# A linear attention stage on one Trainium2 core: layer-norm statistics step by step, and GpSimd's sums of two steps behind one norm

## The chip, the cores and the metric

The kernel runs on one core of a Trainium2 chip, in one launch. The metric is the device time of that launch in microseconds (us). A core has a matrix engine (TensorE, PE in the profile; PEld is its weight load), VectorE (DVE), ScalarE (ACT), GpSimd (POOL) and a queue for DMAs (SP). Each engine runs its own instruction stream in order; semaphores tie the streams together.

## The reference

The program is six blocks on x, 8 batches of 512 tokens with 128 channels: a gated feed-forward with 4-bit blocks, softmax attention, the feed-forward again, a mixture of experts, a linear attention of six layers, and the mixture of experts again. The change lies in the linear attention alone:

```
for l in range(6):
    h = layernorm(x) * gamma[l] + beta[l]          # over the channels
    q, k, v = split(h @ w_qkv[l])
    q = softmax(q, over the 512 tokens);  k = softmax(k, over the channels)
    context = k v^T  (per batch, over channels)
    x = (q applied to context) @ w_out[l] + b_out[l] + x
```

Ahead of it the program applies one more layer norm to x; the stage works on that copy in the tile `ya` and adds x back in the last layer.

## The kernel before, in words

`linear_attn_stage` treats one batch in one layer as a step: 48 steps, step s being batch s % 8 of layer s // 8. A step's input is the output of step s-8. Token tiles have 128 tokens, four to a step. A loop over slots, the same on every engine, holds the software pipeline: in slot s an engine works for step s, s+1, s-1 and so on, always in the order in which the code lists it. The orders are written out by hand; no planner sets them.

VectorE in slot s: the maxima of q (step s, L1439); the addition of the output to `ya` (step s-4, L1446, called the addition below; it waits for the output in PSUM and for `biased`); the maxima of k (step s, L1449, which waits for TensorE's k); then, in odd slots only, `pair_stats(s + 3)`: eight `bn_stats` for steps s+3 and s+4 (L1424); then the norm of step s+2 (four `tensor_scalar` in `ln_apply`, L115), which waits for `rstd_done`; then the scaling of the context (step s-2, L1463) and two reciprocals for step s (L1467, L1468), which wait for ScalarE's exponentials. In layer 0 the statistics are preceded by eight `tensor_scalar` that write `ya`.

GpSimd computes mean and 1/sqrt(var + eps) of a pair of steps from the statistics: `ln_rstd_on_pool`, 21 dependent small instructions, called the chain below (L94 to L107). Besides, once the norm of step s is done, it adds the output bias to that batch's `ya` (L1487, one instruction of 128x512), and in the last layer x too (L1486): called the sums below. Its order is the chain of a pair (s even), the sum of step s-1 having gone before: chain(0), sum(0), chain(2), sum(1), sum(2), chain(4), sum(3), sum(4), and so on, each sum waiting for its norm.

TensorE in slot s: q of step s (L1534), the transposes of step s+1's norm (L1540, which wait for the norm), a product of the context (step s-3, L1545, waits for L1463), k of step s (L1550), another product (L1554), transposes of the exponentials (L1560), the context of step s-2 (L1565), the output of step s-3 (L1573). ScalarE takes two copies, the affine of the norm, the exponentials of q and k (L1506, L1514), and a scaling (L1521).

Of the kernel before, what the change touches and what calls it, by code (L numbers as in the profile page):

```python
# [17 lines left out]
NB = 8  # L18
TPB = 4
# [44 lines left out]
def ln_stats(nc, ch, src, w, summed=False):  # L64


    v, n = nc.vector, src.shape[1]
    if not summed:
        for t in range(n):
            last = v.bn_stats(w["stats"][:, t, :], src[:, t, :])  # L70
        ch.link(last)

    even, odd = w["stats"][:, 0:n, 0:3], w["stats"][:, 0:n, 3:6]
    var, y, s, mean, gap = (w[x][:, 0:n] for x in ("var", "rstd", "tmp", "mean", "gap"))
    v.tensor_tensor(mean, even[:, :, 1], odd[:, :, 1], ALU.add)
    v.tensor_tensor(gap, even[:, :, 1], odd[:, :, 1], ALU.subtract)
    ch.link(v.scalar_tensor_tensor(out=s, in0=even[:, :, 2], scalar=P * LN_EPS, in1=odd[:, :, 2], op0=ALU.add, op1=ALU.add))
    v.tensor_scalar(mean, mean, 0.5, None, ALU.mult)  # L78
    ch.link(v.scalar_tensor_tensor(out=gap, in0=gap, scalar=0.25, in1=gap, op0=ALU.mult, op1=ALU.mult))
    ch.link(v.scalar_tensor_tensor(out=var, in0=s, scalar=1.0 / P, in1=gap, op0=ALU.mult, op1=ALU.add))  # L80

    ch.link(v.tensor_scalar(y.bitcast(I32), var.bitcast(I32), -0.5, RSQRT_SEED, ALU.mult, ALU.add))
    for _ in range(3):
        ch.link(v.tensor_tensor(s, y, y, ALU.mult))
        ch.link(v.scalar_tensor_tensor(out=s, in0=s, scalar=-0.5, in1=var, op0=ALU.mult, op1=ALU.mult))
        ch.link(v.scalar_tensor_tensor(out=y, in0=s, scalar=1.5, in1=y, op0=ALU.add, op1=ALU.mult))
# [24 lines left out]
def ln_apply(nc, src, dst, w, first=0):  # L111

    for t in range(src.shape[1]):
        c = slice(first + t, first + t + 1)
        last = nc.vector.tensor_scalar(dst[:, t, :], src[:, t, :], w["mean"][:, c], w["rstd"][:, c], ALU.subtract, ALU.mult)  # L115
    return last
# [33 lines left out]
def ln_scratch(sb, tag, n=TPB):  # L150
    return {"stats": sb(f"{tag}_stats", [P, n, 6]), **{x: sb(f"{tag}_{x}", [P, n]) for x in ("mean", "gap", "var", "rstd", "tmp")}}
# [1222 lines left out]
def linear_attn_stage(nc, mem, tag):  # L1374
# [4 lines left out]
    with ExitStack() as ctx:  # L1379
        s_ = Scope(nc, ctx, tag)  # L1380
        STEPS = DEPTH * NB
        lnw, lnw_x = [ln_scratch(s_.sb, f"ln{i}", 2 * TPB) for i in range(2)], ln_scratch(s_.sb, "ln_x", NT)
        lnw_x["stats"] = mem["x_stats"]
        ya = s_.sb("y", [P, NT, P])
# [16 lines left out]
        live = lambda s: 0 <= s < STEPS  # L1401
        batch = lambda s: slice((s % NB) * TPB, (s % NB + 1) * TPB)
        SLOTS = range(-1, STEPS + 5)
        tiles = [slice(t * P, (t + 1) * P) for t in range(TPB)]
        with nc.Block() as block:

            @block.sync
            def _(sp):
                clear_spent(sp, mem)

            @block.vector
            def _(dve):
                ch = Chain(dve, chain)
                ln_stats(nc, ch, mem["x"][:], lnw_x, summed=True)

                def pair_stats(s):

                    pair = slice(batch(s).start, batch(s + 1).stop)
                    if s >= NB:
                        dve.wait_ge(y_done, s + 2 - NB)  # L1420
                    else:
                        ch.link(ln_apply(nc, mem["x"][:, pair, :], ya[:, pair, :], lnw_x, pair.start))
                    for t in range(2 * TPB):
                        last = nc.vector.bn_stats(lnw[s // 2 % 2]["stats"][:, t, :], ya[:, pair.start + t, :])  # L1424
                    last.then_inc(stats_done, 1)

                def norm(s):

                    if s >= 4:
                        dve.wait_ge(th_done, s - 3)  # L1430
                    dve.wait_ge(rstd_done, s // 2 + 1)
                    ln_apply(nc, ya[:, batch(s), :], xn[s % 4][:], lnw[s // 2 % 2], s % 2 * TPB).then_inc(xn_done, 1)

                pair_stats(0)
                norm(0)
                for s in SLOTS:
                    if live(s):
                        dve.wait_ge(q_done, s + 1)
                        nc.vector.tensor_reduce(qmax[:, s % 4:s % 4 + 1], qb[s % 2][:], AX.X, ALU.max, negate=True)\  # L1439
                          .then_inc(qmax_done, 1)  # L1440
                    if live(s - 4):
                        dve.wait_ge(o_done, s - 3)
                        dve.wait_ge(biased, s - 3)
                        yb = ya[:, batch(s - 4), :]
                        xb = mem["x"][:, batch(s - 4), :] if s - 4 >= STEPS - NB else yb
                        nc.vector.tensor_tensor(xb, ob[:].rearrange("p (t d) -> p t d", d=P), yb, ALU.add).then_inc(y_done, 1)  # L1446
                    if live(s):
                        dve.wait_ge(k_done, s + 1)
                        nc.vector.tensor_reduce(kmax[:, s % 4, :], kb[:].rearrange("p (t c) -> p t c", c=P), AX.X, ALU.max,  # L1449
                                                negate=True).then_inc(kmax_done, 1)  # L1450
                    if s % 2 == 1 and live(s + 3):
                        pair_stats(s + 3)
                    if STEPS - NB <= s - 5 < STEPS:

                        dve.wait_ge(y_done, s - 4)
                        for t in range(batch(s - 5).start, batch(s - 5).stop):
                            nc.vector.bn_stats(mem["x_stats"][:, t, :], mem["x"][:, t, :])
                    if live(s + 2):
                        norm(s + 2)
                    if live(s - 2):  # L1460
                        dve.wait_ge(m_done, s - 1)
                        c = (s - 2) % 4
                        nc.vector.tensor_scalar(ms[:], mb[:, 0:P], qinv[:, c:c + 1], None, ALU.mult).then_inc(ms_done, 1)  # L1463
                    if live(s):
                        dve.wait_ge(ek_done, s + 1)
                        c = s % 4
                        nc.vector.reciprocal(qinv[:, c:c + 1], qsum[:, c:c + 1])  # L1467
                        nc.vector.reciprocal(kinv[:, c, :], ksum[:, c, :]).then_inc(inv_done, 1)  # L1468

            @block.gpsimd  # L1470
            def _(pool):
                pool.wait_ge(mem["l1_w_loaded"], 16 * 6)
                ch = Chain(pool, pool_chain)

                def pair_rstd(s):
                    pool.wait_ge(stats_done, s // 2 + 1)
                    ln_rstd_on_pool(nc, ch, lnw[s // 2 % 2])
                    nc.gpsimd.sem_inc(rstd_done, 1)  # L1478

                pair_rstd(0)  # L1480
                for s in range(STEPS):

                    pool.wait_ge(xn_done, s + 1)
                    yb = ya[:, batch(s), :]
                    if s >= STEPS - NB:
                        ch.link(nc.gpsimd.tensor_tensor(yb, yb, mem["x"][:, batch(s), :], ALU.add))  # L1486
                    nc.gpsimd.tensor_tensor(yb, yb, mem["boutb"][:, s // NB, :].unsqueeze(1).to_broadcast([P, TPB, P]), ALU.add)\  # L1487
                      .then_inc(biased, 1)
                    if s % 2 == 0 and live(s + 2):
                        pair_rstd(s + 2)  # L1490

            @block.scalar
            def _(act):
# [184 lines left out]
```

## Time and profile before

| what | us |
|---|---|
| median of 3 runs (2016.92 to 2018.34) | 2018.29 |
| the profiled execution's own time | 2015.0 |
| its span | 2013.3 |
| linear attention, first to last of its norms' statistics and additions | from about 1448 to 1775 in the span |
| busy in the span: PE, DVE, POOL, ACT | 1543.9, 1468.0, 1012.1, 885.3 |

The page cuts the span in 40 slices; the linear attention fills slices 29 to 35. The engines' busy digits are:

```
PE   2466799999999999999956564079468888851696
DVE  7989677777777777777757997168577777772484
ACT  1321454444444444444413322057157766620472
POOL 1321266656565656566632324747345555637473
```

A digit is the busy share of a slice in tenths. In a timeline a row is: start, duration, engine, line, operation, output<-input, shapes, count; and in brackets how long the engine had been idle before it and what ended that.

### The profile page before, as it was taken

To read this page: it belongs to the slowest core of one execution; us is meant where nothing else is said; L and a number is where in the kernel's file an instruction comes from. 1 tells how busy PE (TensorE), PEld (TensorE's weight loads), DVE (VectorE), ACT (ScalarE), POOL (GpSimd) and SP (SyncE) were. 2 spreads that over 40 slices of the span, in tenths; PEclk is the share of its full clock that TensorE was granted. 3 is DMA by queue.
4 is the path that set the end of the run, shared out by engine and by line. 5 is a ranking of instruction groups with operands and counts; after the bars stand their busy time and mean duration, and the time that the engine had idled before them with its cause. 6 is when DMAs were issued, how large, how long until landed. Compare 5 with 4: busy or idle time off the path is not lost. (4 is left out here: it accounts for less than half of the span.)

```text
span 2013.3 us, 32025 instructions
## 1 busy us (share of the span) xinstructions
PE 1543.9 (77%) x10355; PEld 869.9 (43%) x10355; DVE 1468.0 (73%) x3104; ACT 885.3 (44%) x2173; POOL 1012.1 (50%) x1324
## 2 busy tenths in 40 slices
PE   2466799999999999999956564079468888851696
PEld 1344233333333333333324344057257767741473
DVE  7989677777777777777757997168577777772484
ACT  1321454444444444444413322057157766620472
POOL 1321266656565656566632324747345555637473
PEclk9888699999999999999977895589779999965798
DMA  6000000000000000000000000233300000002235
GB/s 205 0 0 0 5 23 22 22 22 22 22 22 22 22 22 22 22 22 22 22 16 0 0 1 30 72 87 103 102 1 1 1 2 1 1 20 72 81 105 159
DMA packets 90179, 70.51 MB, mean 35 GB/s; under 512 B 16608, under 2 KB 84640, under 8 KB 90016
## 3 DMA queue, kind: packets, MB, share of 16 engines
q1 hardware_dynamic: 81312, 49.57, 9.1%
q0 software_dynamic: 8704, 18.89, 2.7%
q8 instruction: 87, 1.43, 0.3%
q14 instruction: 76, 0.62, 0.1%
HBM read 29.32 MB, written 22.30 MB: 26 GB/s over the span
## 5 line engine op out<-in xcount | busy, mean ns | idle before, releaser
L662 DVE TENSOR_REDUCE at_nmax<-at_score 128x1 f32<-128x512 f32 x512 | 329.2, 685 | 139.4 <-PE at_score L789 139.4
L753 ACT ACTIVATE at_pT<-at_turned 128x512 f32<-128x512 f32 x512 | 277.9, 595 | 343.0 <-PE at_turned L817 343.0
L648 POOL TENSOR_TENSOR m_rows<-m_rows,at_pT 128x512 f32<-128x512 f32 x256 | 319.4, 1268 | 95.0 <-ACT at_pT L753 95.0
L648 POOL TENSOR_TENSOR m_rows<-at_pT 128x512 f32<-128x512 f32 x128 | 160.2, 1271 | 250.2 <-ACT at_pT L753 250.2
L865 PE MATMUL at_pv<-at_pT,at_v 128*64 128x512 f32 x1024 | 261.7, 611 | 0.4 <-DVE at_oT L692 0.4
L1056 POOL DMA_INDIRECT by_token<-m_ysb,m_dest x144 | 137.8, 957 | 88.0 <-DVE m_ysb L1136 53.9
L1050 POOL DMA_INDIRECT by_expert<-m_rows,m_slot x128 | 123.1, 962 | 70.8 <-issue 38.4
L377 POOL TENSOR_TENSOR f_hq<-f_hg,f_hsc 128x704 f32<-128x704 f32 x32 | 44.3, 1385 | 168.2 <-DVEq L348 168.2
L115 DVE TENSOR_SCALAR la_xn<-la_y,la_ln_mean,la_ln_rstd 128x128 f32<-128x128 f32 x192 | 81.7, 485 | 52.6 <-POOLq L1478 52.6
L450 PE MATMUL f_gate<-m_wguT,f_xqT 128*128 128x352 f32 x128 | 63.9, 588 | 73.1 <-DVEq L343 71.8
L685 DVE RECIPROCAL m_rows<-m_rows 128x256 f32<-128x256 f32 x64 | 111.6, 1743 | 2.9 <-ACT m_rows L759 2.9
L1296 PE MATMUL m_x<-m_ident,m_xin 128*128 128x128 f32 x144 | 23.7, 291 | 116.1 <-DMA m_xin<-by_expert 116.1
L1307 PE MATMUL m_h<-m_w,m_x 128*128 x432 | 109.3, 391 | 3.0 <-DVE m_x L1113 3.0
L838 PE MATMUL at_proj<-m_rows 128*128 128x512 f16 x384 | 108.3, 392 | 4.0 <-DVE at_own L709 2.4
L865 PEld LDWEIGHTS at_pv<-at_pT,at_v 128*64 128x64 f32 x1024 | 56.8, 135 | 117.7 <-issue 117.7
L810 PE MATMUL at_turned<-at_high_q,at_high_k 64*128 64x512 f16 x512 | 102.3, 389 | 0.8 <-ACT at_pT L753 0.5
L789 PE MATMUL at_score<-at_high_k,at_high_q 64*128 64x512 f16 x512 | 99.2, 381 | 2.8 <-DVE at_nmax L662 2.1
L810 PE MATMUL at_turned<-at_low_q,at_high_k 64*128 64x512 f16 x512 | 98.9, 378 | 0.0
L817 PE MATMUL at_turned<-at_mdiag,at_unit 64*128 64x512 f16 x512 | 98.7, 377 | 0.0
L810 PE MATMUL at_turned<-at_high_q,at_low_k 64*128 64x512 f16 x512 | 98.7, 377 | 0.0
L393 ACT ACTIVATE f_silu<-f_gate 128x704 f32<-128x704 f32 x32 | 24.2, 757 | 168.4 <-PE f_up L451 168.4
L1540 PE MATMUL la_th<-m_ident,la_xn 128*128 128x128 f32 x192 | 33.2, 298 | 68.4 <-DVE la_xn L115 66.0
(311 smaller groups left out, 3662.7 us busy)
## 6 DMA issues: line engine op xcount, KB each, us to landing
m_rows<-m_rows SPq DMA_DIRECT2D x512, 32.0 KB, 1.8
m_xin<-by_expert SPq DMA_DIRECT2D x144, 72.0 KB
m_rows<-by_token SPq DMA_DIRECT2D x32, 256.0 KB, 4.6
by_token<-m_ysb,m_dest POOLq DMA_INDIRECT x144, 2.3
m_x<-in_x SPq DMA_DIRECT2D x8, 256.0 KB, 4.8
by_expert<-m_rows,m_slot POOLq DMA_INDIRECT x128, 2.3
out_x<-m_x SPq DMA_DIRECT2D x8, 256.0 KB, 4.1
by_expert<-m_pad SPq DMA_DIRECT2D x18, 72.0 KB, 1.6
```

What stands on the lines that cost most here:

```text
L648: done = nc.gpsimd.tensor_tensor(acc, before, pT[g % 2][:, head, kt, :], ALU.add)
L662: nc.vector.tensor_reduce(nmax[:, head * DH + qt:head * DH + qt + 1], score[head][:], AX.X, ALU.max, negate=True)\
L685: nc.vector.reciprocal(packed, total).then_inc(packed_done, 1)
L753: nc.scalar.activation(pT[g % 2][:, head, kt, :], turned[head][:], ACT.Exp).then_inc(exp_done, 1)
L789: nc.tensor.matmul(score[head][:], high_of[0][g % RING][rows, qt * P:(qt + 1) * P], high_of[1][g % RING][rows, :], start=True, stop=True). ...
L810: nc.tensor.matmul(turned[head][:], k_of[1][k][rows, tile], q_of[0][k][rows, :], start=(n == 0), stop=False)
L817: nc.tensor.matmul(turned[head][:], unit[rows, :], mdiag[rows, :, :].rearrange("p t q -> p (t q)"), start=False, stop=True).then_inc(t_don ...
L838: last = nc.tensor.matmul(proj[:], w[:, w_part, cols], x(x_part, 0, SEQ), start=(i == 0), stop=(i == 2))
L865: last = nc.tensor.matmul(pv[halves[head], :], vv[g % 2][:, kt, halves[head]], pT[g % 2][:, head, kt, :], start=(kt == 0), stop=(kt == TPB ...
L1050: nc.gpsimd.indirect_dma_start(dram_rows, bass.IndirectOffsetOnAxis(slot[:, k, t:t + 1], 0), rows[k][:, t, :], None).then_inc(scattered, 16)
L1056: nc.gpsimd.indirect_dma_start(mem["dram_y_all"], bass.IndirectOffsetOnAxis(dest[j // TPB % DESTS][:, j % TPB:j % TPB + 1], 0), ysb[q % YS ...
L1307: last = nc.tensor.matmul(h[j % 3][:], x16[n % 2][:, x_part, tile], mem["w12_16"][:, w_part, ds(e, 1), :].rearrange("p e h -> p (e h)"), s ...
```

## The change

Statistics are taken by step and no longer by pair. `step_stats(s)` does the four `bn_stats` of one step (in layer 0 with four `tensor_scalar` before them) and is called in every slot for step s+4: in odd slots right behind the addition and ahead of the maxima of k, in even slots behind the maxima of k. It waits for the addition of its own batch. `stats_done` counts steps instead of pairs. GpSimd now runs the chain of a pair (s even), waits for the norm of step s, and then does the sums of steps s-1 and s one after the other; step 47's sum comes last.

```
-                def pair_stats(s):
-                    pair = slice(batch(s).start, batch(s + 1).stop)
+                def step_stats(s):
                     if s >= NB:
-                        dve.wait_ge(y_done, s + 2 - NB)
+                        dve.wait_ge(y_done, s + 1 - NB)
                     else:
-                        ch.link(ln_apply(nc, mem["x"][:, pair, :], ya[:, pair, :], lnw_x, pair.start))
-                    for t in range(2 * TPB):
-                        last = nc.vector.bn_stats(lnw[s // 2 % 2]["stats"][:, t, :], ya[:, pair.start + t, :])
+                        ch.link(ln_apply(nc, mem["x"][:, batch(s), :], ya[:, batch(s), :], lnw_x, batch(s).start))
+                    for t in range(TPB):
+                        last = nc.vector.bn_stats(lnw[s // 2 % 2]["stats"][:, s % 2 * TPB + t, :], ya[:, batch(s).start + t, :])
                     last.then_inc(stats_done, 1)
...
-                pair_stats(0)
+                step_stats(0)
+                step_stats(1)
                 norm(0)
+                step_stats(2)
                 for s in SLOTS:
...                  # maxima of q (s), addition (s - 4)
+                    if s % 2 == 1 and live(s + 4):
+                        step_stats(s + 4)
...                  # maxima of k (s)
-                    if s % 2 == 1 and live(s + 3):
-                        pair_stats(s + 3)
+                    if s % 2 == 0 and live(s + 4):
+                        step_stats(s + 4)
...
                 def pair_rstd(s):
-                    pool.wait_ge(stats_done, s // 2 + 1)
+                    pool.wait_ge(stats_done, s + 2)
                     ln_rstd_on_pool(nc, ch, lnw[s // 2 % 2])
                     nc.gpsimd.sem_inc(rstd_done, 1)
-                pair_rstd(0)
-                for s in range(STEPS):
-                    pool.wait_ge(xn_done, s + 1)
+                def rest(s):
                     yb = ya[:, batch(s), :]
                     if s >= STEPS - NB:
                         ch.link(nc.gpsimd.tensor_tensor(yb, yb, mem["x"][:, batch(s), :], ALU.add))
                     nc.gpsimd.tensor_tensor(yb, yb, ..., ALU.add).then_inc(biased, 1)
-                    if s % 2 == 0 and live(s + 2):
-                        pair_rstd(s + 2)
+
+                for s in range(0, STEPS, 2):
+                    pair_rstd(s)
+                    pool.wait_ge(xn_done, s + 1)
+                    if s:
+                        rest(s - 1)
+                    rest(s)
+                pool.wait_ge(xn_done, STEPS)
+                rest(STEPS - 1)
```

## Rows read from the trace of the kernel before

**Rows 1.** The engines' busy time in stretches: us, busy (instructions) PE, PEld, DVE, ACT, POOL, granted clock, DMA, GB/s.

```profile
1508.35:1701.45 193.10, 162.55 (x1218) 136.10 (x1218) 149.07 (x449) 134.60 (x545) 107.65 (x368) 1.00 0.01 1
1713.52:1726.77 13.25, 10.17 (x78) 8.51 (x78) 10.33 (x29) 8.42 (x35) 9.35 (x26) 1.00 0.01 2
1726.77:1741.39 14.62, 11.63 (x68) 9.98 (x67) 10.40 (x29) 8.67 (x35) 9.25 (x25) 0.78 0.01 1
600.00:700.00 100.00, 100.00 (x730) 39.25 (x728) 76.78 (x111) 49.66 (x97) 61.31 (x50) 1.00 0.09 22
```

**Rows 2.** Waits from 1500 to 1740 us: total us, times, the longest.

```profile
POOL la_ln_mean L94 <- DVE la_ln_stats L1424: 51.2, 19, 2.8
DVE la_xn L115 <- POOLq L1478: 43.6, 20, 2.3
PE la_th L1540 <- DVE la_xn L115: 38.0, 20, 3.0
```

**Rows 3.** Timeline of one pair of slots in the steady part.

```profile
1591.12 1.63 DVE L1424 BATCH_NORM_STATS2 la_ln_stats<-la_y 128x6 f32<-128x128 f32 x8
1592.83 0.24 POOL L94 TENSOR_TENSOR la_ln_mean<-la_ln_stats 128x8 f32<-128x8 f32 x1 [2.84 <-DVE la_ln_stats L1424]
1593.91 0.66 PE L1540 MATMUL la_th<-m_ident,la_xn 128*128 128x128 f32 x4
...
1598.59 2.13 DVE L115 TENSOR_SCALAR la_xn<-la_y,la_ln_mean,la_ln_rstd 128x128 f32<-128x128 f32 x4 [2.17 <-POOLq L1478]
1600.80 1.27 POOL L1487 TENSOR_TENSOR la_y<-la_y,m_boutb 128x512 f32<-128x512 f32 x1 [0.93 <-DVE la_xn L115]
```

**Rows 4.** Timeline of slot 46, near the stage's end, where the norm came early.

```profile
1753.62 1.10 DVE L115 TENSOR_SCALAR la_xn<-la_y,la_ln_mean,la_ln_rstd 128x128 f32<-128x128 f32 x4
...
1754.48 1.02 PE L1534 MATMUL la_q<-la_hT,m_wqkv 128*128 128x512 f32 x2
1755.34 0.60 PE L1540 MATMUL la_th<-m_ident,la_xn 128*128 128x128 f32 x4
1755.54 0.69 DVE L1439 TENSOR_REDUCE la_qmax<-la_q 128x1 f32<-128x512 f32 x1 [0.42 <-PE la_q L1534]
...
1756.14 1.28 POOL L1487 TENSOR_TENSOR la_y<-la_y,m_boutb 128x512 f32<-128x512 f32 x1
1756.15 0.68 DVE L1446 TENSOR_TENSOR m_x<-la_o,la_y 128x512 f32<-128x512 f32 x1
1756.20 0.27 ACT L1498 COPY la_gs<-la_gf 128x128 f32<-128x128 f32 x1 [0.65 <-PE la_gf L1545]
...
1757.09 0.69 DVE L1449 TENSOR_REDUCE la_kmax<-la_k 128x4 f32<-128x512 f32 x1 [0.26 <-PE la_k L1550]
...
1757.84 0.40 ACT L1514 ACTIVATE la_ek<-la_k,la_kmax 128x128 f32<-128x128 f32 x1
...
1759.22 1.18 ACT L1521 ACTIVATE la_eqT<-la_et,la_kinv 128x128 f32<-128x128 f32 x4
...
1759.34 1.02 PE L1534 MATMUL la_q<-la_hT,m_wqkv 128*128 128x512 f32 x2
```

**Rows 5.** Timeline of the norm of step 42, with both of a sum's instructions beside it.

```profile
1719.36 3.22 DVE L115 TENSOR_SCALAR la_xn<-la_y,la_ln_mean,la_ln_rstd 128x128 f32<-128x128 f32 x4 [2.34 <-POOLq L1478]
1720.72 1.26 POOL L1487 TENSOR_TENSOR la_y<-la_y,m_boutb 128x512 f32<-128x512 f32 x1
```

**Rows 6.** Timeline in the attention stage: an addition, statistics behind it, GpSimd beside them.

```profile
355.06 0.68 DVE L698 TENSOR_TENSOR m_x<-at_out,m_x 128x512 f32<-128x512 f32 x1
355.77 0.87 DVE L701 BATCH_NORM_STATS2 m_x_stats<-m_x 128x6 f32<-128x128 f32 x4
356.12 2.50 POOL L648 TENSOR_TENSOR m_rows<-at_pT 128x512 f32<-128x512 f32 x2 [3.48 <-ACT at_pT L753]
```

**Rows 7.** Timeline of the first steps: a chain's start, and layer 0's additional work.

```profile
1482.04 0.24 POOL L94 TENSOR_TENSOR la_ln_mean<-la_ln_stats 128x8 f32<-128x8 f32 x1 [5.67 <-DVE la_ln_stats L1424]
1492.39 2.13 DVE L115 TENSOR_SCALAR la_y<-m_x,la_ln_x_mean,la_ln_x_rstd 128x128 f32<-128x128 f32 x8
```

## The prediction

> **What bounds the kernel now.** The chain of work that ended last reaches back only through the expert stage, so I went by the stage itself. First the busy time by stretches: from 1508 to 1701 us the linear attention runs sixteen equal pairs of slots, 193.10 / 16 = 12.07 us each, and no engine is full: PE 162.55 of 193.10, DVE 149.07, ACT 134.60, POOL 107.65 [rows 1]. So a loop of waits sets the pace. The waits name it: GpSimd waits for the statistics, VectorE's norm waits for GpSimd's chain (20 times, 2.2 us each), TensorE's transposes wait for that norm [rows 2]. The timeline of a pair shows the loop closed [rows 3]: eight statistics 1591.12, chain from 1592.83, norm of the even slot 1598.59 (5.76 us after the chain's start), ended 1600.72, then the transposes, k, k's maxima and behind them the next statistics. A turn is 12.07 us. Two more things are to be seen. That norm takes 2.13 us where the same four instructions take 1.10 in rows 4, because GpSimd's postponed sum starts beside it; with two instructions of a sum beside it it takes 3.22 [rows 5]. And the pair splits unevenly: from the transposes at 1593.91 to the next, behind 1600.72, it is 6.9 us, which leaves 5.2 for the odd slot, whose norm waits for no chain.
>
> What would be the floor? Rows 4 show a slot in which the norm came early: TensorE's q starts at 1754.48 and the next slot's q at 1759.34, 4.86 us, with the transposes 0.86 behind q though their input had been ready at 1754.72. So TensorE's own floor is 4.86 a slot, 9.72 a pair.
>
> **The statistics.** The same 8 x 0.2 us are done per pair (four together 0.87, next instruction 0.78 after their start; eight take 1.63 [rows 3, 6]). What changes is where. Let T be the start of the transposes in an odd slot. By rows 4, q's maxima start at T+0.20, the addition at T+0.81 and it ends at T+1.49, k is ready for its maxima at T+1.75. New: the statistics wait for the addition; rows 6 show that very pattern (355.74 end, 355.77 start), 0.03. They run from T+1.52 to T+2.39, so k's maxima start at T+2.30, 0.55 later than they could, and end at T+2.99; the norm (four instructions, its rstd long there) T+2.91 to 4.09. TensorE wants it at T+4.86: 0.7 of cover. Queued behind the new wait are the maxima, hence ScalarE: its exponentials of k start at T+3.05 (0.06 behind the maxima), its scaling 1.38 later and 1.18 long [rows 4], so it ends at T+5.61, and its first copy of the next slot is due 0.86 behind the next transposes, T+5.72 [rows 4]. That cover is 0.1 only; each tenth beyond it would delay the next slot's first copy by a tenth, and the product that needs it has another 0.4 of slack.
>
> Even slot, T' = T+4.86: maxima of k T'+1.75, statistics T'+2.36, VectorE at the norm at T'+3.14. The chain started at T+2.39+0.08 = T+2.47, so the norm may start at T+2.47+5.76 = T'+3.37: it waits 0.23 instead of 2.17, and ends at T'+4.55 (1.18), 0.3 before TensorE wants it. The saving comes from the chain starting about 2.3 us earlier in its pair, against the point where its norm is read.
>
> **GpSimd's sums.** They move behind the even norm: their start is then T'+4.63, two instructions 0.08 apart end 2.60 later (1.26 each), at T+12.09. The norm of the next odd slot starts at T+9.72+2.91, after them, so the 1.03 us of collision (2.13 - 1.10) go. GpSimd's own loop becomes 5.76 (chain) + 1.18 (norm) + 0.08 + 2.60 + 0.10 (back to the chain, an estimate from the 0.18 that a link costs before a sum) = 9.72, a tie with TensorE's 9.72. `biased` is needed only in slots s+3 and s+4: covered. Two loops that tie never run at exactly the tie; I take 9.8 a pair.
>
> **Does the sum hold the statistics?** The odd slot's statistics (T+1.52 to 2.39) now lie beside the end of the second sum (until T+2.37). Rows 6 show four at 0.87 with a GpSimd instruction starting 0.35 into them, both at normal length; the reverse order, GpSimd first, no row shows. The bound from below is 0; from above, held until the sums end, 0.85 a pair. I take 0, the nearer row. The addition, which has one operand in PSUM, ran 0.68 beside a sum that began first [rows 4]: no cost. The Trainium skill, VectorE: DVE Perf Modes, section "What auto-detection actually checks", says that an instruction with one source, source and destination both in SBUF, qualifies for the mode that uses both read ports, and SBUF — State Buffer, "Who interferes with whom", says that such an instruction and a GpSimd one exclude each other. Taken literally that speaks against this change (the statistics have one source in SBUF); it is the first rival below. For the norm the trace agrees with the exclusion (3.22 against 1.10).
>
> **The start (layer 0, to chain(8) at 1508.35).** Here a step's statistics carry four more `tensor_scalar` (half of the 2.13 for eight [rows 7]), and TensorE is at its lower clock for part of it. Followed slot by slot with the durations above: up to norm(2), ended at 1475.0, nothing changes (one more link, 0.1). The sums then run to 1477.6. Slot 1's four additional instructions fall beside them and are held, so they end at 1478.6 and the statistics at 1479.5: chain(4) at 1479.6 instead of 1482.04 [rows 7]. k's maxima and norm(3) follow to 1481.2; then slot 2: k's maxima to 1484.7 (TensorE at its lower clock), four instructions and statistics to 1486.6, norm(4) to 1487.7, sums to 1490.4. Slot 3 as slot 1: 1.0 and 0.9 behind the sums, chain(6) at 1492.3, which was at 1508.35 - 12.07 = 1496.28. Norm(6) runs 1498.1 to 1499.3 (5.76 and 1.18), the sums to 1502.0, chain(8) starts at 1502.1, against 1508.35. Gain 6.2; bounds 3 (the collisions cost double) and 8 (they cost nothing).
>
> **The steady part.** 16 pairs x (12.07 - 9.8) = 36.3.
>
> **The last layer.** Sums have two instructions each. GpSimd's loop is 5.76 + 1.18 + 0.08 + 0.10 + the sums: 3.94 for three instructions behind norm(40), 5.28 for four behind norm(42) and norm(44): 11.06, 12.40, 12.40, against 12.07, 13.25, 14.62 before [rows 1] (the 14.62 holds a stretch at lower clock). Gains 1.0, 0.85, 2.2. TensorE again idles 2.7 us in these pairs. Behind norm(46): before, 13.33 from chain(46) (1741.39) to norm(47)'s end (1754.72); after, norm(47) is held by four instructions of sums, 12.30 + 1.0 = 13.3: nothing. Sum 4.1.
>
> **Total**: 6.2 + 36.3 + 4.1 = 46.6. The profiled execution took 2015.0, 1.7 above its span: 1968.4. The median of the runs is 3.3 above that execution: 1971.7. The expert stage behind is unchanged.
>
> **Rivals.**
>
> *The sums hold the odd slot's statistics.* GpSimd's loop gets longer by 0.03 + 0.86 + 0.08, less the 0.10: 10.59. Sixteen pairs give 23.7, the start 5.4, the last layer 1.5 (its pairs become 11.9, 13.25, 13.25): 30.6, time 1987.7. For: the skill's rule as quoted. Against: rows 6. 12%.
>
> *The maxima's delay is not covered.* ScalarE's 0.1 or the GpSimd tie slips and the odd slot stays at the 5.2 it has today, some links more: 10.2 to 10.5 a pair. Gain at 10.3: 28.3 + 5.5 + 3.8 = 37.6, time 1980.7. For: two loops without slack. Against: each wait found is under 0.1. 18%.
>
> *No change.* Another wait that the profile hides keeps 12.07, within 0.2% (4 us, about what a measurement can tell): 2018. For: this asks for 2.2 us on some loop where I find none above 9.8. 5%.
>
> *TensorE's clock falls in the fuller stage (the other side).* It was granted 0.78 in the pair from 1726.77 and 0.50 is its lower level (1.2 of 2.4 GHz). At the lower level a slot bound by TensorE doubles: 9.7 more a pair. With a share f of the sixteen pairs there, a pair is 9.8 + 9.7 f; the start and end give back 10.3, so it is slower from 9.8 + 9.7 f > 12.07 + 0.64, f > 0.3. At f = 0.4 a pair is 13.7: 26 lost, 10.3 won, 2034. Against: 1.00 granted at 100% busy for 100 us in the attention stage [rows 1], and all through the steady part; the lower clock came where TensorE idled. 4%.
>
> **How the numbers follow.** The forecast has 61%. Range: below, both loops at exactly 9.72 (1.3 more), the start at 8 (1.8 more), a little for the lower clock in layer 0 ending sooner: 1966. Above, it takes in both partial rivals and a weaker start: 1991. Left out are the last two rivals and little else. Faster 61 + 12 + 18 = 91%, same 5%, slower 4%.
>
> **What would show it.** The distance of two chains (L94 starts) in the steady part near 9.8; the norm's wait for GpSimd from 2.17 down to 0.2 or so; all norms at 1.1 to 1.2 until the last layer, 2 to 3 us for the odd steps there; TensorE's busy share near full at clock 1.00; statistics at 0.86 for four. It is wrong if the pair stays above 10.8, if odd slots show statistics of over 0.3 each beside a sum, if ScalarE becomes the releaser of TensorE's k product, or if the granted clock leaves 1.00 between 1510 and 1690.

## The result and the profile after

The changed kernel takes 1961.59 us (median of 4 runs, 1960.85 to 1963.33) against 2018.32 for the kernel before: ratio 0.9723, 95% interval 0.971 to 0.9736. The direction and the mechanism were forecast, the size was not: 56.7 us won instead of 46.6, and a time 4.4 us below the low end of the stated range.

The steady part, from chain(8) to chain(40), and the three pairs of the last layer, in the columns of [rows 1]:

```profile
1499.64:1655.21 155.57, 155.57 (x1219) 138.67 (x1218) 136.81 (x449) 136.53 (x546) 107.15 (x370) 1.00 0.01 2
1655.21:1665.96 10.75, 10.75 (x88) 9.69 (x87) 9.58 (x30) 9.17 (x39) 7.93 (x24) 1.00 0.00 1
1665.96:1678.12 12.16, 11.46 (x84) 9.28 (x83) 10.36 (x30) 10.16 (x43) 9.26 (x26) 1.00 0.01 2
1678.12:1690.31 12.19, 10.16 (x76) 8.51 (x76) 10.02 (x29) 8.56 (x35) 9.28 (x27) 1.00 0.00 1
```

Sixteen pairs take 155.57 us, 9.72 each, and TensorE is busy for all of it at clock 1.00. VectorE did the same 449 instructions in 12 us less than in [rows 1]; the even norms, without a sum beside them, are 1.02 us shorter each. In the last pairs TensorE is no longer full, and GpSimd's loop sets the pace.

The waits between 1500 and 1655 us, against [rows 2]:

```profile
POOL la_y L1488 <- DVE la_xn L115: 21.6, 16, 1.4
ACT la_gs L1506 <- PE la_gf L1553: 12.8, 32, 0.6
...
DVE la_qmax L1440 <- PE la_q L1542: 7.1, 32, 0.3
ACT la_ek L1522 <- DVE la_kmax L1452: 6.2, 16, 0.4
PEld la_th L1548 <- DVE la_xn L115: 5.4, 16, 0.3
...
DVE la_kmax L1452 <- PE la_k L1558: 4.2, 16, 0.3
POOL la_ln_mean L94 <- DVE la_ln_stats L1423: 4.2, 15, 0.3
```

No wait of a VectorE norm for GpSimd is listed, and no matmul of TensorE waits; a weight load (PEld) waits 0.3 us for the norm, behind matmuls that are still running. Most of the others wait for TensorE. GpSimd waits 0.3 us in each pair for statistics, which is the slack of its loop.

One pair in time order, to be laid beside [rows 3] (the rows that the argument needs; `...` leaves out the rest):

```profile
1595.32 1.28 POOL L1488 TENSOR_TENSOR la_y<-la_y,m_boutb 128x512 f32<-128x512 f32 x1
...
1595.93 0.87 DVE L1423 BATCH_NORM_STATS2 la_ln_stats<-la_y 128x6 f32<-128x128 f32 x4
...
1596.72 0.68 DVE L1452 TENSOR_REDUCE la_kmax<-la_k 128x4 f32<-128x512 f32 x1
...
1596.88 0.21 POOL L94 TENSOR_TENSOR la_ln_mean<-la_ln_stats 128x8 f32<-128x8 f32 x1 [0.28 <-DVE la_ln_stats L1423]
1597.31 1.11 DVE L115 TENSOR_SCALAR la_xn<-la_y,la_ln_mean,la_ln_rstd 128x128 f32<-128x128 f32 x4
...
1597.43 0.37 ACT L1522 ACTIVATE la_ek<-la_k,la_kmax 128x128 f32<-128x128 f32 x1 [0.39 <-DVE la_kmax L1452]
...
1599.26 0.60 PE L1548 MATMUL la_th<-m_ident,la_xn 128*128 128x128 f32 x4
...
1600.12 0.27 ACT L1506 COPY la_gs<-la_gf 128x128 f32<-128x128 f32 x1 [0.16 <-PE la_gf L1553]
...
1601.63 0.86 DVE L1423 BATCH_NORM_STATS2 la_ln_stats<-la_y 128x6 f32<-128x128 f32 x4
...
1602.63 1.11 DVE L115 TENSOR_SCALAR la_xn<-la_y,la_ln_mean,la_ln_rstd 128x128 f32<-128x128 f32 x4
...
1603.82 2.51 POOL L1488 TENSOR_TENSOR la_y<-la_y,m_boutb 128x512 f32<-128x512 f32 x2 [1.35 <-DVE la_xn L115]
...
1604.12 0.60 PE L1548 MATMUL la_th<-m_ident,la_xn 128*128 128x128 f32 x4
```

Norms are 1.11 us both; the odd slot's statistics take 0.87 with a sum beside them that began first; from the chain's start to the norm that reads it are 5.75 us, and the transposes come 4.86 apart.

Where the gain came from, in two profiled executions (2015.0 and 1960.85 us; "lin" ends with the last statistics, 1775.49 and 1723.40):

| stretch | before | after | gain | forecast |
|---|---|---|---|---|
| to chain(8) | 1508.35 | 1499.64 | 8.7 | 6.2 |
| chain(8) to chain(40) | 193.10 | 155.57 | 37.5 | 36.3 |
| chain(40) to chain(46) | 39.94 | 35.10 | 4.8 | 4.1 |
| chain(46) to the end of lin | 34.10 | 33.09 | 1.0 | 0 |
| the expert stage behind | 237.8 | 235.7 | 2.1 | 0 |
| median of the runs above the profiled execution | 3.3 | 0.7 | 2.6 | 0 |

The first row counts from the span's start. The linear attention gave 52.1 instead of 46.6; the other 4.7 lie outside it.

### The profile page after: what moved, and what is told of

Read it like the earlier page. It is cut to its first block and busy times, and to the rows that moved or that the text cites. A ratio compares the mean times of both kernels' runs of the same rounds, so it can differ in the third digit from the quotient of the medians.

```text
span 1959.1 us, 32025 instructions
## 1 busy us (share of the span) xinstructions
PE 1528.9 (78%) x10355; PEld 866.1 (44%) x10355; DVE 1453.2 (74%) x3104; ACT 887.7 (45%) x2173; POOL 1012.4 (52%) x1324
## 5 line engine op out<-in xcount | busy, mean ns | idle before, releaser
L865 PEld LDWEIGHTS at_pv<-at_pT,at_v 128*64 128x64 f32 x1024 | 56.7, 135 | 117.7 <-issue 117.7
L480 PE MATMUL f_down<-m_wdT,f_hqT 128*128 128x128 f32 x384 | 56.0, 300 | 33.6 <-ACT f_hqT L398 33.6
L1117 DVE TENSOR_TENSOR m_dest<-m_xin,m_dump 128x4 int32<-128x4 int32 x36 | 5.5, 153 | 101.0 <-DMA m_xin<-by_expert 101.0
```

Source lines behind the costliest of these rows:

```text
L865: last = nc.tensor.matmul(pv[halves[head], :], vv[g % 2][:, kt, halves[head]], pT[g % 2][:, head, kt, :], start=(kt == 0), stop=(kt == TPB ...
```

## The experiments

Twelve runs of eleven kernels. All but the last two (the second repeat and the mended version) ran on chips on which the kernel before takes 2090 to 2093 us, nearly all of the difference in the expert stages: the one behind the linear attention took 272.5 to 275.8 us there. So totals are compared as ratios to the kernel before on the same chip, and the mechanism by the mean distance of two chains between chain(8) and chain(40), called the pair, and by the length from chain(0) to the last statistics, called lin: 319.8 before, 267.6 after.

**The changed kernel again, twice.**

> The changed kernel itself once more, for what of the 10 us missed is scatter. Theory A (the forecast was off by small terms in the linear attention, and by 2 to 5 us of scatter in the expert stage and in the median): median 1961 to 1963, ratio to before 0.972, the stretch behind the linear attention's last statistics 235 to 238 us. Rival (the change shortens the expert stage too, through the phase in which it is entered): that stretch is 235.7 again within 0.3 us, and in kernels that start it at another time it differs.

> The changed kernel a third time, beside a mended one on the same chip. Theory A (the linear attention is the same to 1 us in every execution; what scatters is the expert stage): pair 9.72, the linear attention from first chain to last statistics 267 to 269 us, ratio to before 0.972 to 0.974. Rival (part of the gain comes and goes with how the stage is entered): the linear attention differs by more than 2 us.

First: ratio 0.9732 (0.9709 to 0.9754), pair 9.72, lin 268.6, expert stage 273.3. Second, on a chip as fast as the first: 1962.25 against 2016.22 (9 runs of before), ratio 0.9733 (0.972 to 0.9746), pair 9.72, lin 267.5, expert stage 237.4. The linear attention repeats to 1.1 us, and all of that 1.1 is the pair from chain(4) to chain(6), for part of which TensorE was at its lower clock in the one execution and not in the other:

```profile
1520.00:1532.28 12.28, 10.67 (x63) 9.64 (x64) 10.11 (x34) 8.19 (x32) 6.83 (x24) 0.72 0.00 1
```

(the first repeat; granted clock 0.72) against, in the profile after of the first section,

```profile
1479.08:1490.22 11.14, 8.54 (x64) 7.09 (x64) 10.12 (x34) 8.09 (x32) 6.80 (x24) 1.00 0.00 1
```

The expert stage's 235.7 came back as 237.4, the length it had before the change (237.8): the 2.1 us there and the 2.6 of the medians are scatter, not the change, as far as one trace of the kernel before can show. With the second repeat's medians the gain is 54.0.

**Only the sums behind the even norm** (statistics by pair; the orders in short form, not the code itself).

```
-                pair_rstd(0); for each s: wait norm(s); sum(s); if s even: chain(s + 2)
+                for s even: chain(s); wait norm(s); sum(s - 1); sum(s)
```

> Statistics by pair as before; only GpSimd's sums of two steps go behind the even norm. Theory A (two loops; the collision of a sum with the even norm costs its whole 1.0 us since that norm is on the loop): pair 11.1 us (5.76 chain to norm, 1.1 norm, 4.19 from its end to the next chain), total about 1997. Rival (the collision only fills time in which TensorE would wait anyway): pair 12.07, total above 2010.

Pair 11.09, lin 295.2, ratio 0.988 (0.9854 to 0.9906). The even norm takes 1.11 instead of 2.13, and 0.98 us comes off the pair, as the loop says:

```profile
1601.46 0.24 POOL L94 TENSOR_TENSOR la_ln_mean<-la_ln_stats 128x8 f32<-128x8 f32 x1 [1.61 <-DVE la_ln_stats L1424]
1607.32 1.11 DVE L115 TENSOR_SCALAR la_xn<-la_y,la_ln_mean,la_ln_rstd 128x128 f32<-128x128 f32 x4 [2.37 <-POOLq L1478]
1608.52 2.50 POOL L1485 TENSOR_TENSOR la_y<-la_y,m_boutb 128x512 f32<-128x512 f32 x2 [1.35 <-DVE la_xn L115]
1610.91 1.63 DVE L1424 BATCH_NORM_STATS2 la_ln_stats<-la_y 128x6 f32<-128x128 f32 x8
1612.62 0.24 POOL L94 TENSOR_TENSOR la_ln_mean<-la_ln_stats 128x8 f32<-128x8 f32 x1 [1.61 <-DVE la_ln_stats L1424]
```

Chain to chain 11.16 here: norm 5.86 behind the chain, 1.11 long, next chain 4.19 behind its end.

**Only the statistics by step** (VectorE as changed; GpSimd's order as before, its wait counting steps).

```
+                    pool.wait_ge(stats_done, s + 2)      # all else of GpSimd as before
```

> Statistics by step as changed; GpSimd's order as before, one sum between the chain and the even norm's end. Theory A: the chain starts 2.47 us behind the odd slot's transposes, norm at 8.23, 2.13 long through the collision, so the pair is 10.4 us, total about 1976 to 1980. Rival (GpSimd's loop with two sums in it sets the pace in the changed kernel, so taking one out is no loss): pair 9.7 to 9.8, total 1960 to 1965.

Pair 10.46, lin 279.6, ratio 0.979 (0.9763 to 0.9817). The even norm is 2.15 long and TensorE waits for it:

```profile
1605.40 2.15 DVE L115 TENSOR_SCALAR la_xn<-la_y,la_ln_mean,la_ln_rstd 128x128 f32<-128x128 f32 x4
1607.60 0.66 PE L1543 MATMUL la_th<-m_ident,la_xn 128*128 128x128 f32 x4 [0.52 <-DVE la_xn L115]
```

So neither part is the whole: alone they bring 0.98 and 1.61 of the 2.35 us a pair; together the sum of 2.59 is cut to 2.35. A pair of 12.07 - 2.59 = 9.48 would lie below TensorE's 9.72, and the next but one experiment shows that TensorE sets the pace there.

**The odd slots' statistics behind k's maxima** (condensed).

```
-                    if s % 2 == 1 and live(s + 4): step_stats(s + 4)      # ahead of the maxima
-                    if s % 2 == 0 and live(s + 4): step_stats(s + 4)
+                    if live(s + 4): step_stats(s + 4)                     # behind them
```

> As changed, but the odd slots' statistics stand behind k's maxima too. Theory A: the chain starts 3.30 us behind the odd slot's transposes instead of 2.47; norm at 9.06 and 1.11 long: pair 10.23 us, total about 1971. Rival (the place ahead of the maxima gives nothing, or costs, since it delays ScalarE by 0.6 us): pair 9.72 or the total at or below 1961.

Pair 10.40, lin 280.9, ratio 0.9792 (0.9766 to 0.9819): the place ahead of the maxima is worth 0.67 us a pair, though it makes ScalarE wait 0.39. The expectation was 0.17 short. The rows show it: the chain starts 3.36 behind the transposes (expected 3.30), and the norm 5.87 behind the chain (expected 5.76), since the chain itself is longer: 5.71 us instead of 5.59. Its third instruction takes 0.29 instead of 0.21, beside a norm of VectorE that began 0.16 before the chain. In the kernel before the two meet in the same way and the chain takes 5.60, but the norm 1.18 instead of 1.10 [rows 4]. What decides which of the two is held is not shown.

```profile
1600.02 0.66 PE L1546 MATMUL la_th<-m_ident,la_xn 128*128 128x128 f32 x4 [0.46 <-DVE la_xn L115]
...
1603.38 0.24 POOL L94 TENSOR_TENSOR la_ln_mean<-la_ln_stats 128x8 f32<-128x8 f32 x1 [0.83 <-DVE la_ln_stats L1423]
...
1609.25 1.11 DVE L115 TENSOR_SCALAR la_xn<-la_y,la_ln_mean,la_ln_rstd 128x128 f32<-128x128 f32 x4 [1.09 <-POOLq L1479]
```

**More work for TensorE, after and before the change.**

```
-                        for t in range(TPB):                      # transposes of the exponentials
+                        for t in [*range(TPB), *range(TPB)]:
```

> The changed kernel with TensorE's four transposes of the exponentials (L1568) done twice, 0.43 us more in a slot. Theory A (TensorE at its floor of 4.86 a slot): pair 9.72 + 0.87 = 10.59 us, total some 16 us longer than the changed kernel. Rival (GpSimd's loop sets the pace, TensorE merely looks busy): pair 9.72 to 9.8.

> The kernel before with the same transposes done twice. Theory A (there the loop of chain, norm and statistics sets the pace and TensorE waits): pair 12.07 to 12.2 us, total within 3 us of before. Rival (TensorE counts there too): pair 12.9.

After the change: pair 10.59 (+0.87, the whole of what was added), lin 282.6, ratio 0.9817 against 0.973. In the kernel before: pair 12.11 (+0.04), ratio 0.999 (0.998 to 1.0). The two stretches:

```profile
1538.00:1707.52 169.52, 169.52 (x1347) 152.65 (x1345) 135.27 (x449) 136.17 (x545) 106.77 (x368) 1.00 0.01 2
```

```profile
1547.04:1740.74 193.70, 173.02 (x1346) 151.32 (x1345) 150.95 (x449) 134.95 (x545) 108.29 (x368) 1.00 0.01 1
```

This is the plainest evidence of which loop sets the pace: in the steady part the same 0.43 us a slot are nearly free in the one kernel and cost in full in the other. Outside it they are not quite free before the change either: lin is 323.7 there, 3.9 more than before, of which 3.1 lie behind chain(46), where the granted clock was 0.95 instead of 0.99. The medians of the two (2092.18 and 2092.87) do not show it.

**A longer and a shorter chain.**

```
-    for _ in range(3):     # ln_rstd_on_pool
+    for _ in range(4):     # and range(2)
```

> The changed kernel with a fourth Newton iteration in GpSimd's chain (four more dependent instructions, 1.13 us). Theory A (GpSimd's loop is 9.45 us with 0.27 of slack under TensorE's 9.72): pair 9.45 + 1.13 = 10.58 us; the linear attention from its first chain to its last statistics some 21 us longer than 267.6 to 268.7. Rival (TensorE alone sets the pace, with more slack elsewhere): pair stays within 0.3 of 9.72.

> The changed kernel with two Newton iterations instead of three (four dependent instructions fewer, 1.13 us). Theory A: pair 9.72 us still, since TensorE is at its floor; only the start and the last layer, which GpSimd's loop sets, give: last pairs 9.72, 11.03, 11.03 instead of 10.75, 12.16, 12.19, the linear attention about 260. Rival (GpSimd's loop is the pace): pair 8.6 to 9.3, the linear attention at or below 250.

Longer: pair 10.53, lin 289.1 (+21.5), ratio 0.9854. The chain's start to its norm grew from 5.75 to 6.85, so 1.10 us were added and not 1.13; 0.81 came through, so GpSimd's loop had 0.29 of slack, as the waits of 0.3 said. Shorter: pair 9.72 exactly as before, last pairs 10.51, 11.08, 11.03, lin 262.5, ratio 0.9723 (0.9706 to 0.9739). TensorE stays at its floor, and only start and last layer give. The first of the last pairs was expected at 9.72: with the chain no longer limiting, the norm stands at its place in VectorE's order, and the three instructions of sums behind it end 0.8 later than the statistics are ready.

**Taking GpSimd out of the last layer.**

```
-                    if s >= STEPS - NB:                               # GpSimd
-                        ch.link(nc.gpsimd.tensor_tensor(yb, yb, mem["x"][:, batch(s), :], ALU.add))
+                        if s - 4 >= STEPS - NB:                       # VectorE, ahead of the addition
+                            ch.link(nc.vector.tensor_tensor(yb, yb, xb, ALU.add))
```

> The changed kernel with the last layer's addition of x moved from GpSimd to VectorE, ahead of the addition of the output, so that a sum is one instruction in every layer. Theory A: last pairs 9.72 like all others, the even norm behind them without its 2.6 us of waiting, the linear attention 258 instead of 267.6 to 268.7, total about 9 us below the changed kernel. Rival (VectorE has no room for 0.7 us more in a slot, or its two-operand addition collides with GpSimd): last layer no shorter.

> Both of the last two: x added on VectorE and two Newton iterations. Theory A: 9.72 a pair throughout, the start shorter by 3 to 4 us, the linear attention 254 to 255. Rival: as for each by itself.

Last pairs 9.72, 9.73, 9.72 as expected; but lin 261.8, not 258, since the stretch behind chain(46) did not shrink (33.3 against 33.1). The even norm's wait there fell from 2.63 to 0.88, yet the norm starts 6.07 behind chain(46) instead of 5.82: its place is set by the chain, and the wait was no time to be won. Norm(47) ends 12.20 behind the chain instead of 12.82, but from there to the last statistics it is 21.06 instead of 20.27, in slots in which VectorE now adds x as well. There the two engines meet again: this addition has both operands in SBUF and is held by a sum that began before it.

```profile
1731.16 1.27 POOL L1489 TENSOR_TENSOR la_y<-la_y,m_boutb 128x512 f32<-128x512 f32 x1 [2.06 <-DVE la_xn L115]
1731.98 1.00 DVE L1448 TENSOR_TENSOR la_y<-la_y,m_x 128x512 f32<-128x512 f32 x1
```

It takes 1.00 where the same instruction takes 0.68 alone, while the addition with its operand in PSUM keeps 0.68 beside a sum [rows 4]. With both x on VectorE and two iterations, lin is 260.6 (254 to 255 was expected): the start gave 1.5 us, not 3 to 4. Ratios 0.9728 (0.9709 to 0.9747) and 0.9715 (0.9698 to 0.9731); at that width they can't be told from the changed kernel's.

**A mended version, beside the changed kernel.**

```
-    for _ in range(3):
+    for _ in range(2):
...
-                    if s >= STEPS - NB:                                          # GpSimd adds x
+                    if s >= STEPS - NB and s not in (41, 43, 45):
...
+                        if s - 4 in (41, 43, 45):                                # VectorE does
+                            ch.link(nc.vector.tensor_tensor(yb, yb, xb, ALU.add))
```

> The changed kernel with two Newton iterations, and the last layer's addition of x on VectorE for steps 41, 43 and 45 alone, so that GpSimd has at most three instructions of sums in a pair. Theory A: GpSimd's loop is 9.45 - 1.13 + 1.3 = 9.6 us, under TensorE's 9.72, so every pair is 9.72; the norms of steps 46 and 47 wait less than in the changed kernel; the linear attention about 258, 9 to 10 us below the changed kernel beside it. Rival (VectorE's additional additions or GpSimd's three instructions push a loop over 9.72): 261 or more.

1956.42 us (1956.12 to 1957.79) against 1962.25 (1959.88 to 1962.79) of the changed kernel on the same chip; ratio to before 0.971 (0.9696 to 0.9723). All runs of the one lie below all runs of the other, so it beats both kernels, by 5.8 us. Its lin is 262.1 against 267.5. The 258 was missed: the pair from chain(4) to chain(6) ran partly at the lower clock (12.24 instead of 11.13), the pair behind chain(40) is 10.52 for the reason seen with the shorter chain, and the stretch behind chain(46) is again 33.1. The shorter chain alone had brought lin to 262.5, so most of the gain is the chain's; spreading x adds 0.4, or 1.5 if the slower pair at the start is left out. What the iteration left out does to the accuracy of the result, no run here measures.

## Why the prediction fell short

*The loop named was right.* Chain, norm, transposes, k, maxima, statistics: taking out its parts one at a time gave 11.09 and 10.46 where its rows said 11.1 and 10.4, and TensorE's added work was nearly free before (0.04 a pair).

*"Statistics", odd slot.* Statistics 0.04 behind the addition, 0.87 long beside a sum that began 0.61 before them (the order that no row of before showed): the first rival is out. Its reading of the Trainium skill went too far. The Trainium skill, VectorE: DVE Perf Modes, section "What auto-detection actually checks", gives where the operands must lie for the two-port mode, but adds that an operation is capped by what the firmware enables; and the Trainium skill's SBUF — State Buffer, "Who interferes with whom", names copy, cast and tensor_scalar as those that can take the shared ports, not these statistics. The trace shows no exclusion for them, while the norm's 2.15 against 1.11, and the two-operand addition's 1.00 against 0.68, are as that section says. The second rival, ScalarE's cover of 0.1, is out too: its copy still waits 0.16 for TensorE. The last two are out as well: the pair is not 12.07, and the granted clock was 1.00 through the steady part.

*"Statistics", even slot.* The norm was to wait 0.23; it starts 0.22 after the place the statistics leave it, 5.75 behind the chain against 5.76.

*"GpSimd's sums": the step that failed first.* "... = 9.72, a tie with TensorE's 9.72." "Two loops that tie never run at exactly the tie; I take 9.8 a pair." It was no tie. Two sums take 2.51, not 2.60: 0.08 between them was read off pairs that have a semaphore wait between their instructions, as x and bias have; two sums of different steps have none, and [rows 6] had shown 2.50 for such a pair. The even norm takes 1.11 once no sum is beside it, not 1.18, as [rows 4] had shown with 1.10. And the chain follows without the 0.10. So GpSimd's loop is 5.75 + 1.11 + 0.08 + 2.51 = 9.45; from chain(6) to chain(8), where it does set the pace, it measures 9.42. TensorE's 9.72 is then alone, and the pair runs at it to the hundredth. Worth 1.2 us in the steady part, and 0.8 in the last layer, whose pairs are 10.75, 12.16, 12.19 against 11.06, 12.40, 12.40.

*"The start": the largest error, 2.5 us.* The order of events held, the durations did not. 0.5 came up to chain(4): VectorE's held instructions ended at 1478.08 instead of 1478.6. 0.4 came behind chain(6), by the terms of GpSimd's loop just named. The other 1.6 lie between: chain(6) was forecast 12.7 behind chain(4), at 1492.3, and came 11.14 behind it, at 1490.22. Slot 2 was costed at TensorE's lower clock, as before, and ran at the upper one. TensorE's k of that slot, before and after, and the granted clock between the two chains of before:

```profile
1484.01 1.91 PE L1550 MATMUL la_k<-m_wqkv,la_hT 128*128 128x128 f32 x8
```

```profile
1481.18 1.16 PE L1558 MATMUL la_k<-m_wqkv,la_hT 128*128 128x128 f32 x8
```

```profile
1482.04:1496.28 14.24, 11.74 (x64) 9.77 (x64) 10.00 (x34) 8.18 (x32) 6.71 (x23) 0.76 0.00 1
```

After the change it was 1.00 between them (above). Ahead of this k TensorE had idled 1.19 us in the changed kernel and 3.53 in the one before. But the changed kernel does not always do so: in the first repeat it idled 2.84, k took 1.91, and chain(4) to chain(6) was 12.25; it was 11.14 and 11.13 in the other two executions, and 12.24 in the mended version. So about 1.1 of the 2.5 us is luck.

*"The last layer", behind norm(46).* The held norm(47) was 2.63 long, ended 12.82 behind the chain instead of 13.3, and 0.5 more came in the slots behind it.

*Outside the stage.* The sum was added to a median 3.3 above the profiled execution; after the change the gap is 0.7, and the expert stage was 2.1 shorter.

*Where the range broke.* Its low end lay 5.7 below the forecast: 1.3 for the two loops at exactly 9.72, 1.8 for the start, the rest for the clock. It allowed nothing for the last layer, where the terms were 1.8 off, and nothing for scatter outside the stage. The stage's own mis-sized terms are 2.5 + 1.2 + 0.8 + 1.0 = 5.5, the scatter 4.7. Scatter alone does not explain it: the ratios of the two repeats, 0.9732 and 0.9733, also lie below 1966 / 2018.3 = 0.974, though that value is within their intervals. The loops and their order were right; the sizes in "GpSimd's sums" and "The start" were not. The tie was taken as a reason to be slower.

What stays open: why TensorE's clock is at its lower level in one slot rather than the next at the start, and why the expert stage differs by 2 us from one execution to the next.

## What to carry to other kernels

Where no engine is full, write down each loop of waits with its length; the change is worth the distance from the loop that sets the pace to the next one, and doubling an operation on the next one, before and after the change, shows which side you are on. A dependent calculation on another engine wants its inputs at the earliest place in the slot, even ahead of work that other engines wait for, as long as these keep some cover. Put GpSimd's large instructions where VectorE does reductions, statistics, or additions from PSUM, not beside its scalings in SBUF; and give a forecast built on one execution the scatter of the runs, on both sides.

## What the runs showed of the hardware

VectorE's `bn_stats` (128x128, SBUF) is not held by a GpSimd addition in either order: in all runs four took 0.85 to 0.88 us, with one beside them or without. An addition on VectorE with both operands in SBUF is held (1.00 against 0.68), one with an operand in PSUM is not (0.68). The holding goes both ways: beside one such addition two GpSimd additions took 2.95 us instead of 2.51. Two independent GpSimd additions of 128x512 take 2.51 us, two with a semaphore wait between them 2.60 to 2.63. TensorE was granted its full clock at 100% busy for 155 us. The kernel before took 2016 to 2018 us in two groups of runs and 2090 to 2093 on other chips. In the traces of the changed kernel nearly all of such a difference lies in the expert stages (235.7 to 237.4 against 273.3 for the last one), and at most 1.1 us in the linear attention.
